# Self-attentions of a Perceiver-like block: scores as 32x64 tiles within a batch, and a new order around them

## The reference

```python
# stage 3: B=8, S=64, H=16 heads of dh=32, no mask
scores = jnp.einsum('bhqd,bhkd->bhqk', q, k) / jnp.sqrt(jnp.float32(dh))
attn = jax.nn.softmax(scores, axis=-1)
ctx = jnp.einsum('bhqk,bhkd->bhqd', attn, v)
attn_out = ctx @ wo.T + bo
# stage 5: q and k after the rotary embedding, causal mask
scores = jnp.einsum('bqhd,bkhd->bhqk', q, k) * SCALE
scores = jnp.where(causal[None, None], -1e+30, scores)
attn = jax.nn.softmax(scores, axis=-1)
out = jnp.einsum('bhqk,bkhd->bqhd', attn, v).reshape(B, S, D)
return out @ Wo.T + bo
```

## Time and profile before

| | us |
|---|---|
| median of 3 runs (lowest, highest) | 3229.72 (3229.62, 3233.3) |
| profiled execution | 3226.25 |
| its span, first to last instruction | 3223.5 |
| TensorE busy in the span | 2926.5 |
| VectorE busy in the span | 1315.4 |
| ScalarE busy in the span | 1023.1 |

### The profile page before, as it was taken

How to read it: one execution, slowest core, us unless ns; L and a number is a source line. 1 busy time by engine, 2 the same in 40 slices (tenths; PEclk the granted TensorE clock), 3 DMA queues, 4 the chain that set the end, 5 groups by cost and what they waited for, 6 DMA issues and landing times.

```text
span 3223.5 us, 37196 instructions
## 1 busy us (share of the span) xinstructions
PE 2926.5 (91%) x15262; PEld 2009.6 (62%) x15262; DVE 1315.4 (41%) x2015; ACT 1023.1 (32%) x1717; POOL 262.1 (8%) x274
## 2 busy tenths in 40 slices
PE   7878899887898779999999969999999999987787
PEld 3336346354583458888888848877877877843432
DVE  3454463646731433333333342444344244336201
ACT  3243122124431433333444322332343233224100
POOL 1100110130000000000000011001101101000000
PEclk9989999997899879999999979999999999988799
DMA  9762894940021022222322210100100100030197
GB/s 381 296 273 98 348 368 181 388 166 27 14 92 52 1 79 91 97 98 91 104 91 100 95 69 20 43 24 20 43 24 21 43 34 26 8 115 36 47 422 300
DMA packets 62272, 388.82 MB, mean 121 GB/s; under 512 B 5696, under 2 KB 12096, under 8 KB 32704
## 3 DMA queue, kind: packets, MB, share of 16 engines
q1 hardware_dynamic: 26640, 190.57, 16.0%
q0 software_dynamic: 29024, 192.23, 15.2%
q10 hardware_dynamic: 6480, 4.20, 0.4%
HBM read 381.72 MB, written 5.24 MB: 120 GB/s over the span
## 4 chain that ended last, share of the span: by engine, by line
PE 74%; DMA 7%; DVE 7%; ACT 5%; issue 4%; POOL 1%; SPq 0%; DVEq 0%; ACTq 0%; POOLq 0%
PE PS L409 10%; PE PS L411 10%; PE PS L410 10%; PE PS L296 4%; PE PS L588 4%; PE PS L1640 4%; DMA PR<-in_ctxN 3%; PE PS L1621 3%; PE PS L1604 3%; PE PS L1623 3%; PE PS L1622 3%; PE PS L1606 3%; PE PS L1605 3%; PE PS L563 2%; DMA ring<-in_experts 2%
## 5 line engine op out<-in xcount | busy, mean ns | idle before, releaser
L409 PE MATMUL PS<-X_high,W_high 128*128 128x512 f32 x576 | 226.5, 393 | 14.5 <-DVE X_low L1123 7.3
L410 PE MATMUL PS<-X_low,W_high 128*128 128x512 f32 x576 | 225.8, 392 | 0.0
L411 PE MATMUL PS<-X_high,W_part 128*128 128x512 f32 x576 | 225.8, 392 | 0.0
L409 PE MATMUL PS<-H_high,W_high 128*128 128x512 f32 x576 | 224.1, 389 | 0.0
L410 PE MATMUL PS<-H_low,W_high 128*128 128x512 f32 x576 | 224.1, 389 | 0.0
L411 PE MATMUL PS<-H_high,W_part 128*128 128x512 f32 x576 | 224.1, 389 | 0.0
L1105 DVE TENSOR_TENSOR W_part<-ring,W_high 128x2048 fp32r<-128x2048 f32 x63 | 147.0, 2333 | 188.6 <-ACT W_high L1071 188.6
L1071 ACT ACTIVATE W_high<-ring 128x2048 fp32r<-128x2048 f32 x71 | 135.1, 1915 | 254.9 <-PE PS L411 254.9
L1804 DVE TENSOR_TENSOR RB<-PS,rows 128x512 f32<-128x512 f32 x104 | 71.8, 691 | 307.3 <-PE PS L1623 307.3
L1111 DVE TENSOR_TENSOR H_low<-T,H_high 128x512 fp32r<-128x512 f32 x144 | 99.7, 692 | 213.8 <-ACT H_high L1092 213.8
L1604 PE MATMUL PS<-C_high,W_part 128*128 128x384 f32 (+2 forms) x512 | 177.5, 347 | 4.9 <-DVE W_part L1776 4.9
(11 more groups left out here) (315 smaller groups left out, 5744.1 us busy)
## 6 DMA issues: line engine op xcount, KB each, us to landing
ring<-in_experts SPq DMA_DIRECT2D x96, 1024.0 KB, 4.9
ring<-in_tiles SPq DMA_DIRECT2D x39, 1024.0 KB, 5.0
RA<-in_ctxT POOLq DMA_DIRECT2D x20, 1792.0 KB, 9.6
RA<-in_ctxT POOLq DMA_DIRECT2D x20, 1536.0 KB, 8.0
T<-in_ctxN POOLq DMA_DIRECT2D x24, 1024.0 KB, 14.2
RA<-in_experts SPq DMA_DIRECT2D x24, 1024.0 KB, 12.8
RB<-in_ctxT POOLq DMA_DIRECT2D x12, 1792.0 KB, 15.6
RC<-in_ctxN POOLq DMA_DIRECT2D x12, 1792.0 KB, 12.5
```

What stands on the lines that cost most here:

```text
L409: pe.matmul(ps, a, xh, start=start, stop=False)
L410: pe.matmul(ps, a, xl, start=False, stop=False)
L411: return pe.matmul(ps, b, xh, start=False, stop=stop)
```

## The change

The score block of a pair no longer covers both batches with each other. For each head and each batch of the pair there is one matmul: 32 rows of contraction (the head's features), 64 queries, 64 keys. It writes PSUM partitions of its batch (u), bank a and columns of chunk g. A pair's scores are then 128 partitions by 16 heads by 64 keys in banks 0 to 3, 256 columns each, half the columns of before. KBD and its copies go. `maxima` in stage 3 takes the maximum from PSUM and subtracts it while copying; in stage 5 it first adds the causal mask. The exponential is one ACTIVATE for a pair, and its sums are a reduction on VectorE. Two products of 64 partitions write the probabilities into the diagonal blocks of `probs`, whose other blocks GpSimd has zeroed once in each stage. Transposes and value matmuls are as before, with the heads in another order.

The order: in stage 3 scores(0), V for two token tiles, scores(1), V for the others, scores(2); in stage 5 K projections and Q rotations in turn, then K rotations and V in turn, then scores(0) to scores(2). Then values(bp) and scores(bp + 3). VectorE does normalise(bp), maxima(bp + 2), and then copies out pair bp - 1.

```diff
-SQ = ["ident", "ones_d", "ones", "blockmask", "causal", "earlier", "rot"]
+SQ = ["ident", "ones_d", "ones", "causal0", "causal1", "earlier", "rot"]
...
+        causal = sq[:, SQ.index("causal0"):SQ.index("causal0") + 2, :].rearrange("p a (b k) -> p (a b) k", k=S)
...
-        KBD = [RB4[0], RB4[1]]
...
+        raw5 = [RB[:, k * 1024:(k + 1) * 1024].rearrange("p (h k) -> p h k", k=S) for k in (0, 1)]
...
-        least = [misc[:, 0:H], misc[:, 16:16 + H]]
+        peak = [misc[:, 0:H], misc[:, 16:16 + H]]
...
-        def attn_pool(pool, at, tag, K, ready):
...
-        def attn_pe(pe, at, tag, Q, V, ready):
...
+        def attn_pool(pool, at, tag):
+            for k, x in enumerate(probs):
+                pool.memset(x, 0.0).then_inc(*at.step(f"{tag}.zero{k}"))
+        def scores_pe(pe, at, tag, Q, K, bp):
+            if bp:
+                pe.wait_ge(*at.done(f"{tag}.raw{bp - 1}"))
+            else:
+                for k in range(G):
                     if bank_reader.get(k):
                         pe.wait_ge(*at.done(bank_reader[k]))
...
             for g in range(KC):
...
+                for a in range(G):
+                    r = slice(a * HD, (a + 1) * HD)
+                    for u in (0, 1):
+                        m = slice((2 * bp + u) * S, (2 * bp + u + 1) * S)
+                        mm = pe.matmul(PS[u * S:(u + 1) * S, a, g * S:(g + 1) * S], Q[r, g, m], K[r, g, m], start=True, stop=True)
+            mm.then_inc(*at.step(f"{tag}.S{bp}"))
...
+        def values_of(pe, at, tag, V, bp):
+            for g in range(KC):
+                if g == 0:
+                    pe.wait_ge(*at.done(f"{tag}.p{bp}"))
+                k = 4 + g % 3
+                if bank_reader.get(k):
+                    pe.wait_ge(*at.done(bank_reader[k]))
+                for a in range(G):
+                    mm = pe.transpose(PS[:, k, a * P:(a + 1) * P], probs[bp % 2][:, G * a + g, :], C["ident"])
+                mm.then_inc(*at.step(f"{tag}.T{bp}.{g}"))
+                bank_reader[k] = f"{tag}.T{bp}.{g}.out"
+            if bank_reader.get(7):
+                pe.wait_ge(*at.done(bank_reader[7]))
+            for g in range(KC):
+                pe.wait_ge(*at.done(f"{tag}.T{bp}.{g}.out"))
+                for a in range(G):
+                    h = G * g + a
+                    mm = pe.matmul(PS[a * HD:(a + 1) * HD, 7, g * P:(g + 1) * P], V[:, bp, h * HD:(h + 1) * HD],
+                                      probsT[:, h, :], start=True, stop=True)
+            mm.then_inc(*at.step(f"{tag}.O{bp}"))
+            bank_reader[7] = f"{tag}.O{bp}.out"
         def attn_act(act, at, tag):
             def exps(bp):
-                for h in range(H):
-                    if h % HALF_H == 0:
-                        act.wait_ge(*at.done(f"{tag}.least{bp}.{h // HALF_H}"))
-                    act.activation(probs[bp % 2][:, h, :], probs[bp % 2][:, h, :], ACT.Exp, bias=least[bp % 2][:, h:h + 1],
-                                   accum_out=sums[bp % 2][:, h:h + 1]).then_inc(*at.step(f"{tag}.exp{bp}.{h // HALF_H}"))
+                act.wait_ge(*at.done(f"{tag}.sub{bp}"))
+                act.activation(raw5[bp % 2], raw5[bp % 2], ACT.Exp, scale=HD ** -0.5).then_inc(*at.step(f"{tag}.exp{bp}"))
...
-                if bp and bp + 1 < NBP:
-                    exps(bp + 1)
...
+                if bp + 2 < NBP:
+                    exps(bp + 2)
...
-        def attn_dve(dve, at, tag, K, ready, O, mask):
...
+        def attn_dve(dve, at, tag, O, mask, values):
             def maxima(bp):
+                x, m = raw5[bp % 2], peak[bp % 2]
+                ps = PS[:, 0:G, 0:KC * S].rearrange("p a (g k) -> p a g k", k=S)
+                dve.wait_ge(*at.done(f"{tag}.S{bp}"))
                 if bp >= 2:
...
+                    dve.wait_ge(*at.done(f"{tag}.p{bp - 2}"))
+                if mask:
+                    dve.tensor_tensor(x.rearrange("p (a g) k -> p a (g k)", a=G), PS[:, 0:G, 0:KC * S],
+                                      causal.rearrange("p g k -> p (g k)").unsqueeze(1).broadcast_to([P, G, KC * S]), ALU.add).then_inc(*at.step(f"{tag}.raw{bp}"))
                     dve.wait_ge(*at.own())
                     dve.tensor_reduce(m, x, AX.X, ALU.max).then_inc(*at.step())
                     dve.wait_ge(*at.own())
...
+                    dve.tensor_tensor(x, x, m.unsqueeze(2).broadcast_to([P, H, S]), ALU.subtract).then_inc(*at.step(f"{tag}.sub{bp}"))
+                    return
+                dve.tensor_reduce(m.rearrange("p (a g) -> p a g", a=G), ps, AX.X, ALU.max).then_inc(*at.step())
+                dve.wait_ge(*at.own())
+                dve.tensor_tensor(x.rearrange("p (a g) k -> p a g k", a=G), ps,
+                                  m.rearrange("p (a g) -> p a g", a=G).unsqueeze(3).broadcast_to([P, G, KC, S]), ALU.subtract).then_inc(*at.step(f"{tag}.sub{bp}"))
+                at.same(f"{tag}.raw{bp}", f"{tag}.sub{bp}")
...
+            def normalise(bp):
+                x, sm = raw5[bp % 2], sums[bp % 2]
+                dve.wait_ge(*at.done(f"{tag}.exp{bp}"))
+                dve.tensor_reduce(sm, x, AX.X, ALU.add).then_inc(*at.step())
+                dve.wait_ge(*at.own())
+                dve.reciprocal(sm, sm).then_inc(*at.step())
+                dve.wait_ge(*at.own())
+                if bp >= 2:
+                    dve.wait_ge(*at.done(f"{tag}.T{bp - 2}.3"))
+                else:
+                    dve.wait_ge(*at.done(f"{tag}.zero{bp}"))
+                for u in (0, 1):
+                    r = slice(u * S, (u + 1) * S)
+                    dve.tensor_tensor(probs[bp % 2][r, :, r], x[r, :, :], sm[r, :].unsqueeze(2).broadcast_to([S, H, S]), ALU.mult).then_inc(*at.step(f"{tag}.p{bp}"))
...
             maxima(0)
+            values(0, 2)
             maxima(1)
+            values(2, 4)
             for bp in range(NBP):
-                for q in (0, 1):
-                    x, sm = probs[bp % 2][:, q * HALF_H:(q + 1) * HALF_H, :], sums[bp % 2][:, q * HALF_H:(q + 1) * HALF_H]
-                    dve.wait_ge(*at.done(f"{tag}.exp{bp}.{q}"))
-                    dve.reciprocal(sm, sm).then_inc(*at.step())
-                    dve.wait_ge(*at.own())
-                    dve.tensor_tensor(x, x, sm.unsqueeze(2).broadcast_to([P, HALF_H, P]), ALU.mult).then_inc(*at.step(f"{tag}.p{bp}.{q}"))
+                normalise(bp)
+                if bp + 2 < NBP:
+                    maxima(bp + 2)
                 if bp:
                     out(bp - 1)
-                    if bp + 1 < NBP:
-                        maxima(bp + 1)
             out(NBP - 1)
...
-            values_pe(pe, at, "s3.v", "s3.wv", X3, (4, 5, 6, 7))
-            attn_pe(pe, at, "s3.at", Q3, V3, [f"s3.q.{c}.out" for c in range(KC)] + [f"s3.v.{c}.out" for c in range(4)])
+            for due in at.last(*(f"s3.q.{c}.out" for c in range(KC)), *(f"s3.k.{c}.out" for c in range(KC))):
+                pe.wait_ge(*due)
+            scores_pe(pe, at, "s3.at", Q3, K3, 0)
+            values_pe(pe, at, "s3.v", "s3.wv", X3, (4, 5, 6, 7), range(0, 2))
+            scores_pe(pe, at, "s3.at", Q3, K3, 1)
+            values_pe(pe, at, "s3.v", "s3.wv", X3, (4, 5, 6, 7), range(2, 4))
+            scores_pe(pe, at, "s3.at", Q3, K3, 2)
+            for bp in range(NBP):
+                values_of(pe, at, "s3.at", V3, bp)
+                if bp + 3 < NBP:
+                    scores_pe(pe, at, "s3.at", Q3, K3, bp + 3)
...
+            attn_dve(dve, at, "s3.at", O3, False, lambda a, b: values_dve(dve, at, "s3.v", V3, "bv3", (4, 5, 6, 7), range(a, b)))
...
-            linear_pe(pe, at, "s5.k", [("s5.wk", N5)], (4, 5, 6, 7), range(KC))
-            rotate_pe(pe, at, "s5.qr", Q5, [f"s5.q.{c}.out" for c in range(KC)], (0, 1, 2, 3))
-            rotate_pe(pe, at, "s5.kr", K5, [f"s5.k.{c}.out" for c in range(KC)], (4, 5, 6, 7))
-            values_pe(pe, at, "s5.v", "s5.wv", N5, (0, 1, 2, 3))
-            attn_pe(pe, at, "s5.at", Q5, V5, ["s5.qr.done"] + [f"s5.v.{c}.out" for c in range(4)])
+            for c in range(KC):
+                linear_pe(pe, at, "s5.k", [("s5.wk", N5)], (4 + c,), (c,))
+                rotate_pe(pe, at, "s5.qr", Q5, "s5.q", (c,), 0)
+            for c in range(KC):
+                rotate_pe(pe, at, "s5.kr", K5, "s5.k", (c,), 4)
+                values_pe(pe, at, "s5.v", "s5.wv", N5, (0, 1, 2, 3), range(c, c + 1))
+            pe.wait_ge(*at.done("s5.kr.done"))
+            scores_pe(pe, at, "s5.at", Q5, K5, 0)
+            scores_pe(pe, at, "s5.at", Q5, K5, 1)
+            scores_pe(pe, at, "s5.at", Q5, K5, 2)
+            for bp in range(NBP):
+                values_of(pe, at, "s5.at", V5, bp)
+                if bp + 3 < NBP:
+                    scores_pe(pe, at, "s5.at", Q5, K5, bp + 3)
...
+            attn_dve(dve, at, "s5.at", O5, True, lambda a, b: None)
...
```

More of the change, by code:

```diff
@@ L1244, in attn_pe @@
-        def attn_pe(pe, at, tag, Q, V, ready):
-            def scores(bp):
-                pe.wait_ge(*at.done(f"{tag}.kb{bp}"))
```

(55 more changed lines are left out.)

56 lines of the change are left out of this document (12 added, 44 removed).

## The result

The changed kernel takes 3191.88 us, median of 4 runs (3186.24 to 3195.83), against 3229.67 us (3227.86 to 3233.3, 4 runs) for the kernel before on the same chip: a ratio of 0.988, 95% interval 0.9863 to 0.9898. It is faster by 1.0 to 1.4%. The profiled execution took 3191.41 us.

The account below looks back on a forecast made before the run. Inside the attentions ScalarE's exponentials, with VectorE between them, set the pace; VectorE becomes the bound. Savings 20.0 (stage 3) + 13.6 (stage 5) - 3.0 - 2.4 (clock) = 28.2 from 3229.7: 3201.5 us, range 3194 to 3211.

Parts of the forecast that it names:

- Rival (e): VectorE's four-dimensional PSUM reads take twice 1.22 us in eight exposed operations; 18.4 us saved, 3211.3 us; chance 0.05.
- the price of a score call: TensorE's 64 score instructions a pair on 32x64 tiles: 50 ns each, 3.2 us a pair, 5.0 at low clock.
- So the scores themselves save nothing: TensorE's scores: 3.2 us a pair now against 3.4 us at full clock before, so no gain from them.
- stage 3: key projection's end to V's end, with two calls: Stage 3, TensorE: a 0.9 us bubble, two score calls and V's matmuls, from 1053.1 to 1074.2.
- stage 3: tail, with 1.2 for the clock: Stage 3 after the last probabilities: transposes, copies, values 3.2 us, last copy 0.8, plus 1.2 for half clock.
- stage 5: V's end to the last product: Stage 5: scores, then VectorE's maxima and normalising in series, from 2933.2 to the last probabilities at 2969.8.
- stage 5: low clock before maxima(3): Stage 5: TensorE at half clock after idling ends values(0) and scores(3) 3.0 us after VectorE wants them; charged 3.0.
- (b): Rival: full clock and 39 ns a score instruction in both stages; 37.1 us saved, 3192.6 us; chance 0.08.
- (a): Rival: low clock everywhere, delaying stage 3's scores(3) and both tails; 21.7 us saved, 3208.0 us; chance 0.2.
- (c): Rival: 98 ns a score instruction, 3.0 us more a call; 11 us saved, 3218.5 us; chance 0.04.
- (d): Rival: small score tiles do not run side by side, 8.1 us a call; 3236 us, slower by 6; chance 0.03.
- New waits: Stage 3: output copies behind the next maxima make values(1) wait for bank 7 until 1088.2; hidden, no cost.

Follow-up runs that it names:

- out_first: Changed kernel with VectorE's output copy put ahead of the next maxima instead of behind them; 3187.98 us, one run.
- old_order: Changed kernel's new score and softmax forms, put back in the order of the kernel before; 3217.66 us, ratio 0.9969 to the kernel before.
- scores_x2: Changed kernel with every score product computed twice, 128 instructions a call, same result; 3197.48 us, one run.
- scores_x4: Changed kernel with every score product computed four times, 256 instructions a call, same result; 3219.54 us, ratio 0.9965 to the kernel before.

## Why the prediction was right, and where it failed

*The bound before, and VectorE after: right.* Exponential 1.06 us (forecast 1.04), full VectorE operations 1.22 to 1.23, products 1.23 each as taken. Normalising came to 4.1 us against 3.85: from V's end to the last product stage 3 took 23.0 us, the forecast 22.3. Rival (e) did not happen: the reads of PSUM in the four-dimensional view took 1.22 to 1.23.

*The step that failed is the price of a score call.* The step "With 64 columns it is nearer the first; I take 50 ns, 3.2 us a pair, ends 2.5 and 6.2" took as its lower bound a row where a different tile ran, 128 rows by 32 columns. Measured: 13 ns and 0.84 us a call, a quarter of the 3.2 us. At low clock the prediction took 5.0 us; scores(2) of stage 5 ran at a granted clock of 0.50 and took 1.29. "So the scores themselves save nothing" falls with it. The Trainium skill, TensorEngine Tiling (Array Packing), Performance Considerations, whose charge of 60 cycles (25 ns, an estimate of 36 us saved) the prediction weighed against its rows, was nearer for the sum, but is also twice what the trace shows. Rows 7 and 9 could not show the low end. Both rows have more columns in each instruction, 128 and 416 against 64, and nothing in them excluded less than 39 ns. So 39 ns was an example, and no lower bound.

Term by term, in the profiled executions:

| term | forecast | measured | difference |
|---|---|---|---|
| stage 3: key projection's end to V's end, with two calls | 21.1 | 16.7 | -4.4 |
| stage 3: V's end to the last product | 22.3 | 23.0 | +0.7 |
| stage 3: tail, with 1.2 for the clock | 5.2 | 4.1 | -1.1 |
| stage 5: V's end to the last product | 36.6 | 34.3 | -2.3 |
| stage 5: low clock before maxima(3) | 3.0 | 0 | -3.0 |
| stage 5: tail, with 1.2 for the clock | 5.2 | 4.1 | -1.1 |

The differences add up to 11.2 us: 9.7 in the first, fourth and fifth rows, 2.2 in the tails, and 0.7 the other way. The first and fourth rows are calls: 2.35 us each in stage 3; in stage 5 scores(0), and 0.8 for a wait of maxima(1) that did not come, less 0.9 for VectorE. The fifth is the low clock, and it hangs on the same price. The granted clock was indeed 0.50 there, as feared. These are windows of 6 us of the changed kernel in stage 5, columns as in the earlier trace rows:

```profile
2922.00:2928.00 6.00, 1.29 (x64) 1.10 (x64) 5.86 (x7) 2.11 (x2) 0.00 (x0) 0.50 0.01 3
2928.00:2934.00 6.00, 4.15 (x28) 3.79 (x32) 5.80 (x6) 2.23 (x4) 0.00 (x0) 0.50 0.00 0
2934.00:2940.00 6.00, 4.28 (x108) 3.40 (x100) 5.76 (x6) 2.79 (x6) 0.00 (x0) 0.88 0.00 0
```

But values(0) and scores(3) together needed 6.4 us, not 10.5, and were done before VectorE wanted them, as a row of TensorE and one of VectorE show:

```profile
2935.32 0.96 PE L1248 MATMUL PS<-T 32*64 32x64 f32 x64
...
2937.66 1.23 DVE L1300 TENSOR_TENSOR RB<-PS,sq 128x1024 f32<-128x1024 f32 x1
```

Values(0) took 5.5 us from start to start (2929.85 to 2935.32), as forecast for low clock. Scores(3) took 0.96 in place of 5.0; the granted clock had risen to 0.93 by then, but with the 1.29 us of scores(2) it would also have been in time. So the charge went with the call's size. In stage 3, where the prediction charged nothing for the clock, TensorE was idle for 3.86 us before the first transposes, and they took 3.52 us at a granted clock of 0.53, hidden behind VectorE. That leaves the tails: pair 2's transposes stand just ahead of the last pair's; they took 3.48 us, also hidden, and the last pair's 2.00 at full clock. The 1.2 us charged twice were not paid.

*Rivals.* (b), full clock and 39 ns, at 3192.6, was the nearest, by luck. Its clock was right only in the tails and its price three times too high. It also saves on three calls in stage 3 and two in stage 5, while by the prediction's own schedule only two calls stand on the path in stage 3 (scores(2) ends at 1077.4, ahead of maxima(2) at 1078.9). (a) was right that the granted clock is 0.50 behind idle stretches, wrong that it costs. (c) and (d) are excluded by the 13 ns. The median's saving of 37.8 us lies between the span's 33.9 and the stretches' 39.1. That the varying wait of the earlier stage makes the difference is likely, but the executions other than the profiled ones have no trace to show it.

*New waits.* Values(1) did wait for bank 7 (idle 1.19 us in stage 3 and 2.45 in stage 5, released by the copy L1330), and it was hidden: out_first takes that wait away and changes nothing. *The order*, whose parts the prediction did not price apart, turned out to be most of it: 26.8 of 39.1 us (14.5 + 12.3), by old_order, on top of the new forms.

## What to carry to other kernels

Where a small tile's instruction price decides a range and the nearest rows are of another tile, the low end stays open: set it by what the rows exclude, not by the cheapest row at hand. When the pace-setting engine has changed, ask again what it does for the engine that is now free: here sixteen short exponentials with their sums on ScalarE beat one long one with a sum on VectorE. And when score blocks become cheap, issue them before the work that they used to queue behind: here that was worth 26.8 us, where the new forms in the old order were worth 12.3.

## What the runs showed of the hardware that was not expected

- Products on 32x64 tiles with 64 columns run at 12 to 13 ns an instruction at a granted clock of 1.00: 64 in 0.84 us from start to start, 186 in 2.22 us. At 0.50, 128 took 2.26 us (scores_x2) and 186 3.50 us (scores_x4), 18 to 19 ns. A 128x128 transpose takes 125 ns (16 in 2.00 us).
- In runs of such short instructions TensorE stood still for 1.2 to 3.3 us with no other engine named: after 186 instructions, and in stage 3 of scores_x4 after 244. In scores_x4 each further standstill came 255 or 256 MATMUL rows of any kind after the last, six times out of six. A wait of 1.3 us in between did not move the place (128 and 58 in scores_x2), but scores_x2 had one standstill in stage 5 and none in stage 3. What supplies the instructions at this point was not tested. The changed kernel's calls of 64 show no such gap.
- A product of 64 partitions by 1024 columns takes VectorE as long as one of 128 partitions, 1.23 us. The same product takes GpSimd 2.94 us, and VectorE's product that starts just ahead of it stays at 1.22. One of 64x512 that VectorE starts while GpSimd's product runs takes 1.43 us in place of 0.68, four times out of four.
